# Slot numbers of a mixture-of-experts layer: threshold count and mask penalty added on TensorE, minimum on VectorE

## The reference

```
x = x + attn(layernorm(x))      # two-level wavelet filter bank round a linear attention, then a layer norm
x = x + ffn(layernorm(x))

ffn:  scores = sigmoid(h @ gate_w.T)                  # 2048 tokens, 16 experts
      topk_score, topk_ids = top_k(scores.T, 256)     # every expert picks its 256 best tokens
      eo  = down(silu(g(h[ids])) * up(h[ids])) * topk_score
      out = zeros.at[topk_ids].add(eo) + shared expert(h)
```

## Time and profile before

| | us |
|---|---|
| median of 3 runs | 236.66 |
| lowest and highest of them | 234.34, 237.17 |
| the profiled execution | 234.46 |
| its span, first to last instruction | 232.7 |
| TensorE busy | 193.6 |
| VectorE busy | 134.5 |
| ScalarE busy | 75.6 |
| GpSimd busy | 107.2 |

### The profile page before, as it was taken

The page is one execution under the profiler, slowest core; times in us unless marked ns, Lnnn a source line. Parts: engine busy times, 40 slices in busy tenths (PEclk is TensorE's granted clock), DMA queues, the critical chain, the costliest instruction groups (busy, mean ns, idle before and its releaser), DMA issues.

```text
span 232.7 us, 3493 instructions
## 1 busy us (share of the span) xinstructions
PE 193.6 (83%) x1248; PEld 162.3 (70%) x1248; DVE 134.5 (58%) x387; ACT 75.6 (33%) x176; POOL 107.2 (46%) x109
## 2 busy tenths in 40 slices
PE   7579999997799788996579999999999888999000
PEld 7446969997695355654468999999998777899000
DVE  3889996599516989979755444444444434444000
ACT  1584201247843201120004444444444343444100
POOL 7500280345200000000277677878888788655650
PEclk9967999999755999999679999999999999999755
DMA  6999994000008200110132233333233333223321
GB/s 210 408 418 419 412 415 170 3 0 4 1 0 290 93 3 0 45 48 0 45 97 55 51 48 38 48 35 48 42 46 48 44 45 49 23 23 27 32 23 11
DMA packets 11585, 22.20 MB, mean 95 GB/s; under 512 B 1456, under 2 KB 8752, under 8 KB 11440
## 3 DMA queue, kind: packets, MB, share of 16 engines
q1 hardware_dynamic: 5936, 17.52, 19.4%
q0 software_dynamic: 5632, 4.46, 14.5%
HBM read 17.65 MB, written 4.33 MB: 94 GB/s over the span
## 4 chain that ended last, share of the span: by engine, by line
PE 32%; DVE 25%; DMA 14%; POOL 12%; issue 9%; ACT 4%; POOLq 1%; DVEq 0%; ACTq 0%
DMA out_dram<-area,rows 11%; POOL out_dram L414 8%; PE bank L1195 6%; PE bank L1196 5%; PE bank L1179 5%; PE bank L1030 4%; DVE stats L551 4%; POOL hT L402 3%; DVE area L757 2%; PE bank L1073 2%; PE bank L929 2%; POOL rstd L379 2%; PE bank L1022 2%; DVE area L632 2%; DVE mean_var L554 2%
## 5 line engine op out<-in xcount | busy, mean ns | idle before, releaser
L402 POOL DMA_INDIRECT hT<-h_rows,rows x32 | 33.1, 1036 | 62.6 <-DVE rows L835 53.2
L414 POOL DMA_INDIRECT out_dram<-area,rows x32 | 50.8, 1587 | 19.2 <-DMA out_dram<-area,rows 10.1
L879 DVE SCALAR_TENSOR_TENSOR area<-bank,consts,sgate 128x256 f32<-128x256 f32 x64 | 30.8, 482 | 34.0 <-ACT sgate L530 33.8
L530 ACT ACTIVATE sgate<-bank,consts 128x256 f32<-128x256 f32 x64 | 30.0, 469 | 62.8 <-PE bank L1196 62.8
L1195 PE MATMUL bank<-area,wT 128*128 128x256 f32 x128 | 39.4, 390 | 3.6 <-issue 2.9
L1179 PEld LDWEIGHTS bank<-wT,area 128*128 128x128 f32 x256 | 38.2, 191 | 3.3
L1179 PE MATMUL bank<-wT,area 128*128 128x128 f32 x256 | 38.6, 275 | 0.0
L1196 PE MATMUL bank<-area,wT 128*128 128x256 f32 x128 | 38.1, 379 | 0.0
L1196 PEld LDWEIGHTS bank<-area,wT 128*128 128x128 f32 x128 | 24.3, 190 | 3.3
L1195 PEld LDWEIGHTS bank<-area,wT 128*128 128x128 f32 x128 | 19.3, 191 | 6.1 <-issue 4.7
L379 POOL TENSOR_TENSOR rstd<-var_eps,half_pow 128x4 f32<-128x4 f32 (+1 forms) x10 | 12.5, 1250 | 20.8 <-DVE var_eps L556 20.8
(11 more groups left out here) (158 smaller groups left out, 249.5 us busy)
## 6 DMA issues: line engine op xcount, KB each, us to landing
wT<-in_weights_dram SPq DMA_DIRECT2D x16, 768.0 KB, 18.1
h_rows<-hrow SPq DMA_DIRECT2D x2, 576.0 KB, 4.1
x_tok<-in_x_dram SPq DMA_DIRECT2D x2, 512.0 KB, 4.4
x_tok<-in_down_b_dram SPq DMA_DIRECT2D x1, 1024.0 KB, 7.1
out_dram<-x SPq DMA_DIRECT2D x4, 256.0 KB, 2.2
hT<-h_rows,rows POOLq DMA_INDIRECT x32, 2.6
out_dram<-area,rows POOLq DMA_INDIRECT x32, 3.4
sh_wT<-in_shared_dram SPq DMA_DIRECT2D x1, 384.0 KB, 5.9
```

Source lines behind the costliest of these rows:

```text
L402: pool.indirect_dma_start(out=gath[:, e % GBUF, c, :], out_offset=None, in_=h_rows[:, :], in_offset=bass.IndirectOffsetOnAxis(ap=rows[:, g ...
L414: pool.indirect_dma_start(out=out_rows, in_=eo[:, e % 2, c, :], in_offset=None, out_offset=bass.IndirectOffsetOnAxis(ap=rows[:, g, c, k:k ...
L530: act.activation(sgate_e[:, q % SGB, :], up_bank(q)[:, CAP:2 * CAP], ACT.Silu, bias=biasT[:, 1, j, e:e + 1]).then_inc(s_sil, 1)
L879: dve.scalar_tensor_tensor(hidden[:, e % 2, j, :], up_bank(q)[:, 0:CAP], biasT[:, 0, j, e:e + 1], sgate_e[:, q % SGB, :], ALU.add, ALU.mul ...
```

## The change

TensorE takes over two additions. A new constant `apart_bf`, with -4096 on the diagonal, is multiplied with both masks and added to the positions in bank 5. VectorE sums `pair` of mask 0 over the eight row pairs (`over_row`), and one multiplication with ones adds that count to the second half of bank 5. The eight multiplications into bank 6 and `above_no` go. The slot is then the minimum over both halves of bank 5, plus 4096: a marked token's own position, or a number of 4096 or more. The list of tokens is the same as before.

```diff
@@ gpsimd, set-up @@
             pool.tensor_copy(ident_bf[:, :], ident[:, :])
+            link(pool.memset(apart_bf[:, :], 0.0))
+            pool.affine_select(out=apart_bf[:, :], in_=apart_bf[:, :], compare_op=ALU.not_equal, fill=-UNSET, base=0,
+                               pattern=[[-1, P]], channel_multiplier=1)
@@ vector @@
                               ALU.add).then_inc(s_mask, 1)
-            dve.wait_ge(s_above, 1)
-            link(dve.tensor_scalar(above_no[:, :], bank[6][:, 0:E], -UNSET, None, ALU.add))
+            dve.wait_ge(s_mask, 1)
+            dve.tensor_reduce(over_row[:, :], pair[:, 0, :, :].rearrange("p k e -> p e k"), AX.X, ALU.add).then_inc(s_over, 1)
             dve.wait_ge(s_pos, 1)
-            dve.scalar_tensor_tensor(rank[:, 0, :], bank[5][:, 0:256], -UNSET, mask[:, 0, :], ALU.add, ALU.mult)
-            link(dve.tensor_tensor(by_tile(rank[:, 1, :]), by_tile(bank[5][:, 256:512]), per_expert(above_no[:, :], NT),
-                                   ALU.add))
-            link(dve.tensor_tensor(rank[:, 1, :], rank[:, 1, :], mask[:, 1, :], ALU.mult))
-            link(dve.scalar_tensor_tensor(slot[:, :], rank[:, 0, :], UNSET, rank[:, 1, :], ALU.add, ALU.add))
+            link(dve.tensor_scalar(rank[:, 0, :], bank[5][:, 0:256], UNSET, None, ALU.add))
+            link(dve.scalar_tensor_tensor(slot[:, :], bank[5][:, 256:512], UNSET, rank[:, 0, :], ALU.add, ALU.min))
@@ tensor, positions() @@
                 pe.wait_ge(s_mask, 1)
-                for k in range(BLK):
-                    last = pe.matmul(bank[6][:, 0:E], ones_bf[:, :], pair[:, 0, k, :], start=(k == 0), stop=(k == BLK - 1))
-                last.then_inc(s_above, 1)
...
+                pe.matmul(bank[5][:, :], apart_bf[:, :], mask[:, :, :].rearrange("p x n -> p (x n)"), start=False,
+                          stop=False, skip_group_check=True)
                 for x in range(2):
...
-                last.then_inc(s_pos, 1)
+                pe.wait_ge(s_over, 1)
+                pe.matmul(bank[5][:, 256:512].rearrange("p (m e) -> p m e", e=E), ones_bf[:, :],
+                          over_row[:, :].unsqueeze(1).to_broadcast([P, 2 * BLK, E]), start=False, stop=True,
+                          skip_group_check=True).then_inc(s_pos, 1)
```

More of the change, by code:

```diff
@@ L69, in wavelet_attention_moe @@
         before_bf = sb("before_bf", [P, P], BF16)
+        apart_bf = sb("apart_bf", [P, P], BF16)
+        over_row = sb("over_row", [P, E], BF16)
         digit = sb("digit", [P, HI, 8], U16)
@@ L160, in wavelet_attention_moe @@
         thr16 = sb("thr16", [P, E], U16)
-        above_no = sb("above_no", [P, E])
         sh_hid = sb("sh_hid", [P, 2, 2, 512])
@@ L223, in wavelet_attention_moe @@
         s_mask = sem("s_mask")
-        s_above = sem("s_above")
+        s_over = sem("s_over")
         s_shg = sem("s_shg")
@@ L1089, in positions @@
                           skip_group_check=True)
+                pe.matmul(bank[5][:, :], apart_bf[:, :], mask[:, :, :].rearrange("p x n -> p (x n)"), start=False,
+                          stop=False, skip_group_check=True)
                 for x in range(2):
                     for s in range(1, BLK):
-                        last = pe.matmul(out_of[:, x * BLK + s:(x + 1) * BLK, :, :], ones_bf[:, :],
-                                         pair[:, x, 0:BLK - s, :].unsqueeze(2).to_broadcast([P, BLK - s, 2, E]),
-                                         start=False, stop=(x == 1 and s == BLK - 1), skip_group_check=True)
-                last.then_inc(s_pos, 1)
+                        pe.matmul(out_of[:, x * BLK + s:(x + 1) * BLK, :, :], ones_bf[:, :],
+                                  pair[:, x, 0:BLK - s, :].unsqueeze(2).to_broadcast([P, BLK - s, 2, E]),
+                                  start=False, stop=False, skip_group_check=True)
+                pe.wait_ge(s_over, 1)
+                pe.matmul(bank[5][:, 256:512].rearrange("p (m e) -> p m e", e=E), ones_bf[:, :],
+                          over_row[:, :].unsqueeze(1).to_broadcast([P, 2 * BLK, E]), start=False, stop=True,
+                          skip_group_check=True).then_inc(s_pos, 1)
             def beside(r):
```

## The result

The changed kernel takes 234.09 us in the median of 20 executions (230.62 to 238.75), the kernel before 235.57 in 20 others (233.54 to 237.56). The ratio given with them is 0.9893, interval 0.9857 to 0.9929: about 2.5 us faster, where 0.7 was forecast. That ratio leaves out executions over 1.5% above the fastest of the same kernel, which keeps 10 of the changed kernel's 20 and 17 of the other's, so that it leans to the changed kernel's low half. With all executions of both kernels that this study has (65 before, 26 changed) the means are 235.26 and 233.94: 1.3 us faster, interval 0.5 to 2.2, a ratio of 0.9944 (0.9908 to 0.9980). The 0.7 us lie inside this interval and outside the other. Both intervals take the executions as independent of each other, and the second mixes chips.

The account below looks back on a forecast made before the run. Between masks and first gather it saw a relay, TensorE to about 103.94 us, then VectorE alone. Terms -0.79 + 0.11 = -0.68 us took the three runs' median of 236.66 to 236.0 us, range 233.3 to 237.6.

Parts of the forecast that it names:

- VectorE behind the positions: Lines 798 to 803: four instructions taking 1.71 us become two linked ones taking 0.92; gain 0.79 us, bounds 0.69 to 0.81.
- The sum over pairs: VectorE ahead of the positions: 0.29 us inside its 1.03 us wait, costing nothing unless over 1.3 us.
- TensorE: Multiplications between the masks and the positions: signal to VectorE comes 0.11 us later, bounds 0.10 and 0.35.
- Sum: From the masks to the first gather: -0.79 + 0.11 = -0.68 us, ends -0.71 and -0.34.
- GpSimd's set-up: A memset and a select ahead of line 379, +0.52 us, covered by a 1.25 us wait for VectorE; 0.73 left.
- Rival A: Gain isn't passed on, by the branch through line 721 or pacing behind the gather; 236.7 us from the median; chance 0.10.
- Rival B: Clock falls later, into the stage behind line 1166, costing up to 3.4 us; 239.4 us from the median; chance 0.07.
- Rival C: Clock doesn't fall in front of the spread (line 1149): 0.31 us more gain, 235.7 us from the median; chance 0.11.
- the prediction's own last sign of being wrong: Prediction fails if the runs move by something that lies outside 102 to 114 us altogether.
- the range is that spread, moved: Range 233.3 to 237.6 us: lowest run less 0.71 and 0.31, highest run without gain plus 0.4 of the clock rival.

Follow-up runs that it names:

- e8: Changed kernel with the penalty added in two multiplications of -2048 in place of one of -4096; one execution, 232.82 us.
- e7: Changed kernel with dummy multiplications in all TensorE idle places, four more linked VectorE instructions, 12 dummies for 5 ahead of the first table; median 232.95 us.
- e1: Kernel before with only the constant built on GpSimd in the set-up, unused; median 235.32 us, ratio 1.0109 to the kernel before.
- e3: Changed kernel with dummy multiplications in some of TensorE's idle places; median 231.65 us, ratio 0.9934 to the kernel before.
- e2: Kernel before with dummy multiplications in some of TensorE's idle places; median 231.02 us, ratio 0.9907 to the kernel before.
- e4: Changed kernel run again without any edit, for a second profile; median 233.58 us, ratio 1.0007 to the kernel before.
- e5: Kernel before with dummy multiplications in all of TensorE's idle places up to the experts; mean 232.62 us over 12 executions.
- e6: Changed kernel with dummy multiplications in all of TensorE's idle places up to the experts, 5 ahead of the first table; mean 230.12 us.
- e9: Kernel before with all dummy multiplications, unchanged, a second time; mean 231.69 us over 6 executions.
- e11: Changed kernel with all dummy multiplications a second time; mean 231.30 us over 5 executions, a sixth of 257.41 left out.

## Why the prediction was right in its step and wrong in the whole

- **VectorE behind the positions:** forecast -0.79, measured 1.71 - 0.92 = -0.79. By the prediction's estimate from the Trainium skill ("VectorE: DVE Perf Modes", section on the TRN2 errata) it would have been -0.65. The trace again doesn't agree with a lower fixed cost for instructions without PSUM: both new ones, which read PSUM, start 0.46 apart like those that didn't.
- **The sum over pairs:** 0.38 us and not 0.29, still inside the wait, which is 1.30 us.
- **TensorE:** forecast +0.11. From the pair sum's start to VectorE's next step it is 2.01 after 1.95, +0.06. The wait for the sum cost nothing, and e8 shows the price per 512 columns.
- **Sum:** forecast -0.68, with ends of -0.71 and -0.34; measured -0.73 in the profile, 0.02 beyond the nearer end.
- **GpSimd's set-up:** its wait for VectorE fell from 1.25 to 0.58 (forecast 0.73) and went on covering it.
- **Rival A:** out by e7. The branch of the chain through line 721 was no wait. The chain of the changed kernel shows it:

```profile
102.47 1.24 DVE area L811
103.71 0.02 issue
103.73 0.07 DVE area L817
103.80 0.09 issue
103.89 0.05 DVEq L725
103.94 0.94 issue
104.88 1.22 DVE area L811
```

VectorE was busy with line 817 meanwhile:

```profile
103.73 1.23 DVE L817 TENSOR_TENSOR area<-area,token_no 128x2048 f16<-128x2048 f16 x1
104.88 1.22 DVE L811 TENSOR_TENSOR area<-area,digit 128x2048 f16<-128x2048 uint16 x1
```

By this reading VectorE's sequencer passes that wait 0.94 us ahead of the instruction, in both kernels. Before, this moment happened to fall 0.01 us behind the end of TensorE's line 1039; now it doesn't, and the chain runs through VectorE.

- **Rival B:** real, 1.7 us in e1 and about 3.0 in e3, 2 of 13 profiles, one with the edit on VectorE and TensorE and one without. It is part of the spread; that the change makes it no more frequent isn't shown by two cases.
- **Rival C:** in the changed kernel's profile the spread took 0.79 us as before. It happened in full only with dummies (0.48 in e2; 0.71 in e4 without them), which makes S to G 0.33 shorter, as its price of 0.31 said.

**What failed** is the step from the sum to the kernel's time. The sum has terms from 102 us to the first gather alone and puts all that lies ahead at nothing, the set-up by its cover, the slow clock behind 62 us without a word. The ratio says 2.5 us faster, and of the profiles' 3.34 us 2.95 lie ahead of the pair sum. It is the prediction's own last sign of being wrong: the runs moved by something that lies outside 102 to 114 us. In its place the runs showed that M comes anywhere from 99.15 to 102.10 us without dummies, 2.35 us apart in two executions of the changed kernel. Whether all of this is the executions' spread, or a part comes from the set-up, stays open (e1).

The base was off too: "the range is that spread, moved", with the spread of three executions (2.83 us) and their median, 236.66. The median of 20 was 235.57, so the base was 1.1 us too high. The slow stretch behind 62 us was not treated as a thing that comes and goes, though it costs more (5.14 for 2.89 us on one line) than the whole edit. The 0.50 in that stretch could have been read beforehand, since the page's clock row has it; rival B was built on the slow stretch at 112 us alone. Executions of either kernel spread over 7 to 8 us in this study. The measured ratio of 0.9893 therefore holds the edit's 0.7 us and, most likely, which executions it counts; the second part is argued from the comparison of all executions and from e4, and no run isolates it. What remains between 0.7 and the 1.3 us of all executions is 0.6 us, with a standard error of 0.43, and so not told from nothing; a small effect of the change on where the slow stretches fall is neither shown nor excluded.

**A version that beats both:** the changed kernel with all dummies, mean 230.66 us over 11 executions (without the one of 257.41), ratio to the kernel before 0.9821 (0.9754 to 0.9888) and 0.9865 (0.981 to 0.9919). The dummies are worth more than the edit, 3 us in e2's means. The Trainium skill ("TensorE: Matmul & The Clock Gate", Part 1) has activity lift the throttled state and idleness bring it back; the rows at 62 to 74 us and at 104 to 123 us agree, where dummies in the idle places kept the clock at 1.00 in e5 and e6. The falls near 69 us in e9 and e11 stand behind dense work and aren't told by it.

## What to carry to other kernels

Read the granted clock of every stretch before adding up a change: where it stands at half in front of dense TensorE work, that stretch can differ from one execution to the next by more than a small edit is worth, as it did here. Judge an edit of under a microsecond by the interval between two fixed instructions in several profiles of both kernels, not by medians of whole executions. And take a wait in the chain that ends long before its instruction starts, on an engine that shows no idle time, for the sequencer running ahead.

## What the runs showed of the hardware that was not expected

- The same 24 multiplications of 16 columns took 5.14 us at a granted clock of 0.50 (before), 2.89 with a clock of 0.91 to 0.94 over most of them (changed) and 2.75 at 1.00 (e2).
- Two executions of one program differed by 2.35 us in when the thresholds stood (99.15 and 101.50).
- A scatter of 128 rows that adds landed after 5.14 us once, with 3.2 to 3.3 for its neighbours.
- GpSimd's scatters keep a period of 6.39 to 6.44 us while gathers share its queue, and of 5.30 to 5.72 us afterwards, in every profile, but for the 7.27 us of e5's late scatter. F to L is 93.16 to 93.62 us in twelve of thirteen profiles. The granted clock from 125 to 200 us was 1.00 in all of them, so no run shows what a slow clock there would cost.
